# A two-layer FFN and adapter network on one core: part of the mixing done by quarters between product groups

## What is computed

```python
def L0_cond(x, weights, condition):
    return jnp.einsum('bct,bcd->bdt', x, weights[condition])        # x: (32, 64, 1024), weights: (16, 64, 64)
def L0_ffn(x, w12, b12, w3, b3):
    x1, x2 = jnp.split(jnp.einsum('bsk,mk->bsm', x, w12) + b12, 2, axis=-1)
    return jnp.einsum('bsm,nm->bsn', silu(x1) * x2, w3) + b3
def L1_cond(x, idx, W, lora_A, lora_B):
    xr = jnp.einsum('bsi,bir->bsr', x, lora_A[idx])
    return jnp.einsum('bsi,io->bso', x, W) + jnp.einsum('bsr,bro->bso', xr, lora_B[idx])
def L1_ffn(x, W_org, lora_down, lora_up, lora_keys, Wq):
    ...  # base product, softmax router over 8 experts, rank 64 each
x = x + L0_ffn(L0_cond(x, L0_cond_weights, itok), ...)
x = x + L1_ffn(L1_cond(x, itok, ...), ...)
```

## Time and profile before

| | us |
|---|---|
| median of 3 runs | 981.84 (981.64 to 982.62) |
| the profiled execution | 981.73 |
| its span | 980.0 |

### The profile page before, as it was taken

One profiled execution on the slowest core, in us unless ns is written; L12 is line 12 of the kernel. 1 busy time (PEld: TensorE's weight loads), 2 busy tenths in 40 slices (PEclk: granted clock), 3 DMA queues, 4 the chain that ended last, 5 costly groups with the idle time before them and its releaser, 6 DMA issues.

```text
span 980.0 us, 12537 instructions
## 1 busy us (share of the span) xinstructions
PE 975.1 (99%) x4790; PEld 807.9 (82%) x4790; DVE 799.2 (82%) x644; ACT 406.7 (41%) x373; POOL 37.7 (4%) x63
## 2 busy tenths in 40 slices
PE   9999999999999999999999999999999999999998
PEld 8888888888888888888898888888888888888886
DVE  3977877998867898778866888779987779887887
ACT  6553553453344433332355545444334453423322
POOL 2600000000000000000100000000000000000001
PEclk9999999999999999999999999999999999999999
DMA  9032044024013102240531210620340131012013
GB/s 353 2 100 94 1 160 183 20 81 179 24 44 119 53 1 65 97 162 11 192 142 43 86 44 9 236 99 28 116 159 1 43 129 44 1 65 86 1 44 129
DMA packets 23194, 84.43 MB, mean 86 GB/s; under 512 B 2706, under 2 KB 6818, under 8 KB 17250
## 3 DMA queue, kind: packets, MB, share of 16 engines
q1 hardware_dynamic: 20880, 75.77, 21.2%
q0 software_dynamic: 2112, 7.36, 1.9%
q10 hardware_dynamic: 146, 0.52, 0.2%
HBM read 75.25 MB, written 8.39 MB: 85 GB/s over the span
## 4 chain that ended last, share of the span: by engine, by line
PE 99%; DVE 0%; issue 0%
PE banks L695 32%; PE banks L696 31%; PE banks L697 31%; PE banks L787 3%; PE banks L751 1%; PE banks L770 1%; PE banks L821 0%; PE banks L800 0%; PE banks L816 0%; DVE r L1088 0%; DVE r L959 0%; PE banks L810 0%; PE banks L806 0%
## 5 line engine op out<-in xcount | busy, mean ns | idle before, releaser
L695 PE MATMUL banks<-s_hi,t_hi 128*128 128x512 f32 x1344 | 525.4, 391 | 0.0
L696 PE MATMUL banks<-s_lo,t_hi 128*128 128x512 f32 x1344 | 523.1, 389 | 0.0
L697 PE MATMUL banks<-s_hi,t_lo 128*128 128x512 f32 x1344 | 522.9, 389 | 0.0
L695 PEld LDWEIGHTS banks<-s_hi,t_hi 128*128 128x128 f32 x1344 | 252.2, 188 | 54.7 <-issue 1.5
L697 PEld LDWEIGHTS banks<-s_hi,t_lo 128*128 128x128 f32 x1344 | 252.3, 188 | 53.1
L696 PEld LDWEIGHTS banks<-s_lo,t_hi 128*128 128x128 f32 x1344 | 252.3, 188 | 51.1
L957 DVE TENSOR_TENSOR t_lo<-w,t_hi 128x1024 fp32r<-128x1024 f32 x134 | 160.0, 1219 | 9.4 <-ACT t_hi L890 9.4
L1083 DVE TENSOR_TENSOR r<-banks,r 128x1024 f32<-128x1024 f32 x102 | 123.5, 1220 | 46.3 <-PE banks L697 39.8
L890 ACT CAST t_hi<-w 128x1024 fp32r<-128x1024 f32 x134 | 136.5, 1048 | 51.2 <-PE banks L697 42.3
L862 ACT CAST s_hi<-st 128x2048 fp32r<-128x2048 f32 x40 | 76.5, 1913 | 183.0 <-PE banks L697 130.6
L957 DVE TENSOR_TENSOR s_lo<-st,s_hi 128x2048 fp32r<-128x2048 f32 x40 | 91.6, 2291 | 46.0 <-ACT s_hi L862 46.0
(11 more groups left out here) (84 smaller groups left out, 429.4 us busy)
## 6 DMA issues: line engine op xcount, KB each, us to landing
w<-w_up_in SPq DMA_DIRECT2D x16, 1024.0 KB, 5.0
w<-w_base_in SPq DMA_DIRECT2D x10, 1024.0 KB, 4.8
w<-w_down_in SPq DMA_DIRECT2D x8, 1024.0 KB, 5.1
r<-x_t_in SPq DMA_DIRECT2D x8, 1024.0 KB, 6.2
w<-w_lin_in SPq DMA_DIRECT2D x8, 1024.0 KB, 5.1
out_t<-r POOLq DMA_DIRECT2D x14, 512.0 KB, 4.8
we<-w_expin_in SPq DMA_DIRECT2D x10, 512.0 KB, 4.7
r<-x_pairs_in SPq DMA_DIRECT2D x8, 512.0 KB, 9.2
```

The source lines that it names most:

```text
L695: pe.matmul(out, w_hi, x_hi, start=start, stop=False, skip_group_check=True)
L696: pe.matmul(out, w_hi, x_lo, start=False, stop=False, skip_group_check=True)
L697: return pe.matmul(out, w_lo, x_hi, start=False, stop=stop, skip_group_check=True)
```

## The change

The mixing of pairs 6 and 7 of the first half, and of all pairs of the second, is done *by quarters* (`mixing_between`): each k is four matmuls, for the two samples j (rows 64j to 64j+63 of the array) and the two halves q of the 128 columns of x (PSUM partitions 64q to 64q+63), with 64 moving columns. Sample j goes to its own bank. The zero quarters of `mix` are no longer read.

Where it stands: the first half's pairs 6 and 7 come after group 1 of product 0; the second half's pairs two at a time after the last group of products 2, 3 and 5 of the first half's expup, and after group 2 of product 6. ACT's copies move along. Product 0 of the first half starts after pair 5; for this, the first two chunks' `s_hi` and `s_lo` are made ahead of the rest (`first_ready`). DVE makes the first half's sums T1 and T2 ahead of S1 and S2, and the second half's T1 and T2 within product 0 of its up0 and no longer beside the last expup product. SP loads x pairs 4 to 7 of the second half in a row, ahead of the weight block "12".

```diff
-    if n == 0:
-        to = 0
-    elif n < LAST and PRODUCTS[n + 1][1] == 0:
+    if kind == "up0" and i == 0:
+        to = s
+    elif n < LAST and PRODUCTS[n + 1][1] == 0 and kind_of(n + 1) != "up0":
         to = s + 1
...
+MIX_LATE = (6, 7)
+MIX_BETWEEN = {(2, 3): (0, 1), (3, 3): (2, 3), (5, 3): (4, 5), (6, 2): (6, 7)}
+def mix_bank(h, c):
+    return ((0, 2, 4, 6, 4, 6, 4, 6) if h == 0 else (4, 6, 4, 6, 0, 2, 0, 2))[c]
...
                 elif h + 1 < HALVES:
-                    load_x(h + 1, 4)
-                    load_x(h + 1, 5)
+                    for c in range(4, PAIRS):
+                        load_x(h + 1, c)
                     load_w(s + 1, "12")
-                    load_x(h + 1, 6)
-                    load_x(h + 1, 7)
                     load_w(s + 1, "22")
...
+            def mixing_between(h, pairs):
+                for c in pairs:
+                    bank = mix_bank(h, c)
+                    wait_mixing(h, c)
+                    if h == 0 or c in (2, 3, 6, 7):
+                        pe.wait_ge(mixed_copied, h * PAIRS + c - 1)
+                    else:
+                        wait_taken(pe, phase_of(h - 1, "expup", 1 if c < 4 else 4), 2 * (c % 2))
+                    for k in range(K):
+                        for q in range(2):
+                            for j in range(2):
+                                rows, cols = slice(j * S, (j + 1) * S), slice(q * S, (q + 1) * S)
+                                last = pe.matmul(banks[cols, bank + j, k * S:(k + 1) * S],
+                                                 x_pair(c)[rows, k * P + q * S:k * P + (q + 1) * S],
+                                                 mix[rows, c, rows], start=True, stop=True, skip_group_check=True)
                     last.then_inc(mixed_full, 1)
...
-                    pe.wait_ge(s_ready, n + 1)
+                    if n == 0:
+                        pe.wait_ge(first_ready, 1)
+                    else:
+                        pe.wait_ge(s_ready, n + 1)
...
+                        if n == 0 and p == 2:
+                            pe.wait_ge(s_ready, 1)
...
+                    if n == 0 and g == 1:
+                        mixing_between(0, MIX_LATE)
+                    if kind == "expup" and h + 1 < HALVES and (i, g) in MIX_BETWEEN:
+                        mixing_between(h + 1, MIX_BETWEEN[i, g])
...
+                between = kind == "expup" and h + 1 < HALVES
+                if between and i == 6:
+                    s_split(n + 1)
+                    copy_mixed(h + 1, 4)
+                    copy_mixed(h + 1, 5)
                 t_split(n, 0)
+                if between and i in (3, 4):
+                    for c in MIX_BETWEEN[i - 1, 3]:
+                        copy_mixed(h + 1, c)
+                if between and i == 6:
+                    copy_mixed(h + 1, 6)
+                    copy_mixed(h + 1, 7)
```

More of the change, by code:

```diff
@@ L825, in tensor_engine @@
                 h, kind = STAGES[s]
-                if kind == "up0" and i == 0:
-                    mixing(h)
+                if n == 0:
+                    mixing()
                 if kind == "lin" and i < 2:
@@ L862, in s_split, with t_split @@
                 act.copy(s_hi[:, slot, cols], s_source(n)).then_inc(s_hi_done, 1)
-            def t_split(beside, when):
+            def t_split(beside, when, which=(0, 1, 2, LORA)):
                 for n, j in t_halves(beside, when):
+                    if j not in which:
+                        continue
                     s, i = PRODUCTS[n]
@@ L951, in scalar_engine @@
                 t_split(n, 2)
-                if kind == "expup" and i == 6 and h + 1 < HALVES:
-                    mixing(h + 1)
+                if n == 0:
+                    for c in MIX_LATE:
+                        copy_mixed(0, c)
         def vector_engine(dve):
@@ L1178, in copy_coef @@
                                 coef_bank[:, 0:KE * BH]).then_inc(coef_ready, 1)
-            t_split(-1, 0)
-            s_split(0)
+            t_split(-1, 0, (0,))
+            slot, cols = s_place(0)
+            first, rest = slice(cols.start, cols.start + 2 * TN), slice(cols.start + 2 * TN, cols.stop)
+            dve.wait_ge(first_hi_done, 1)
+            lo(s_lo[:, slot, first], s_source(0)[:, 0:2 * TN], s_hi[:, slot, first]).then_inc(first_ready, 1)
+            dve.wait_ge(s_hi_done, 1)
+            lo(s_lo[:, slot, rest], s_source(0)[:, 2 * TN:], s_hi[:, slot, rest]).then_inc(s_ready, 1)
+            t_split(-1, 0, (1,))
             dve.wait_ge(consts_made, 5)
@@ L1199, in vector_engine @@
                     take(dve_own(n)[1])
-                    if i not in (3, 4):
+                    if i not in (3, 4) and (i < 6 or h + 1 == HALVES):
                         t_split(n, 0)
@@ L1230, in vector_engine @@
                     sum_y(s, 2)
+                if n == 0:
+                    for what in t_sums_beside(n):
+                        t_sum(*what)
                 for name in {0: ("S1", "S2"), 2: ("S4",), 3: ("S3",)}.get(i, ()):
```

80 lines of the change are left out of this document (51 added, 29 removed).

## The result

The changed kernel took 975.88 us in the median (975.6 to 976.59, six runs), the kernel before 981.82 in the same rounds. The ratio is 0.9939, with a 95% interval from 0.9926 to 0.9952: 6.0 us less, 0.6%. The forecast was 975.9, within a range from 974.4 to 982.0.

The account below looks back on a forecast made before the run. PE, busy 975.1 of 980.0 us, bounds the kernel. Removed mixing -17.9, quarters +9.5, places +2.0 and waits +0.5 give -5.9 us: 975.9 from 981.84, range 974.4 to 982.0.

Parts of the forecast that it names:

- What is removed: Full-size mixing on PE: the second half's eight pairs (14.29 us) and the first half's last two (3.60) go, 17.89 us.
- The price of a pair: Mixing by quarters: 0.95 us a pair if the step follows the columns, between 0.90 and 1.79; ten pairs 9.5 us.
- A place: Changing the array's shape around each of five places of two pairs: 0.40 us each (0.29 to 0.50), 2.0 us in all.
- Waits: PE waits at second pairs, the first product's start, product 2 and x loads: 0.5 us in all, bounds 0 and 1.5.
- The forecast's covers: Slack before PE would wait for DVE: 0.2 us at first product, 0.3 and 1.8 at product 2 of each half.
- The sum: Whole kernel: -17.9 + 9.5 + 2.0 + 0.5 = -5.9 us, from 981.84 to 975.9.
- Rival 1: Mixing quarters on PE: records, not columns, set the pace, 1.79 us a pair, +2.5 us, 984.3; chance 0.14.
- Rivals 2 and 4: Mixing quarters: a four at 0.07 to 0.09 us, 977.5 to 981 (0.15); or overlap only in twos, 984.3 or above (0.04).
- Rival 3: DVE late at product 2 of a half, or x pair 6 late, by 1 to 4 us: 977 to 980; chance 0.07.
- What would show it: New profile: 640 quarter records, places of 2.2 to 2.4 us, next half's product near 500.7; DVE waits would say otherwise.

Follow-up runs that it names:

- full_between: Changed kernel with its ten moved pairs as full 128x128 matmuls again, at the new places; 982.02 us, ratio 1.0001 to the kernel before.
- the two orders in turn: Changed kernel with its quarter matmuls reordered: all eight k of one quarter, then the next (997.13 us), or two quarters taking turns (982.76 us).
- all_quarters: Changed kernel with the first half's pairs 0 to 5 by quarters too and s_hi ahead of the weight cast; 981.91 us.
- one_place_quarters: Changed kernel with the second half's eight quartered pairs in one place after the last product, copies, sums and loads ordered as before; 982.5 us.
- one_place_quiet: one_place_quarters with the changed kernel's x loads, weight blocks 12 and 22 loaded after the last pair, weight sums in product 0; 980.38 us.
- weights_late: Changed kernel with the second half's weight blocks 12 and 22 asked for only after its last pair is mixed; 975.98 us, ratio 0.9927.
- halves_in_turn: Changed kernel with quarters two at a time, the two row halves in turn (order q, k, j); 982.76 us, ratio 0.9998.

## Why the prediction was right, step by step

- **What is removed**, 17.89 us: right in size. The first half gave 3.38 of its 3.60, since pair 4 began at 13.73 for 13.54, named as a wait for its load, which landed at 13.46 for 13.29. The changed kernel asks for these loads as before, and in the kernels here that keep pairs 0 to 5 at full size the same load landed between 13.12 and 14.19. So this is the execution and not the change.
- **The price of a pair**, 0.95 us between 0.90 and 1.79: measured 0.93. The argument was that L770 and L787 share a step because they share a stream, so that half the columns give half the step. full_between and the two orders in turn agree with both parts of it: the same matmuls give nothing at full size, and give it back when fewer quarters run together. The 55 ns for a weight load of 64 columns is only the columns' share: the record is 0.135 us long, as the rows of 32 and 128 columns would give (110 + 32 x 0.85 = 137 ns), so the loads fit under the step because they overlap.
- **A place**, 0.40 us between 0.29 and 0.50: measured 0.37, and 0.36 with one pair. Row halves and column halves together cost about what row halves cost alone in the earlier trace rows. The products behind a place were not in the sum, some 0.04 us each.
- **Waits**, 0.5 us between 0 and 1.5: about 0.8, and not where they were looked for. The forecast's covers held. DVE's half of s_lo was ready by 15.60 + 1.2 = 16.8, before PE came for it at 17.38; the t_lo of product 2 was ready at about 39.59 + 1.2 = 40.8 (forecast 40.9), and PE came at 41.4; that of the second half at 518.46 + 1.2 = 519.7 (forecast 520.7), and PE came at 521.9. X pairs 6 and 7 landed at 491.5 and 492.8, for a bound of 496.0, and PE wanted the first at 495.9. The 0.6 in the last place was missed: it is the late block of instructions, which the forecast had no term for.
- **The sum**: -17.9 + 9.3 + 1.9 + 0.2 (pair 4) + 0.6 (pause) + 0.2 (products behind the places) = -5.7, for a forecast of -5.9. Small misses of opposite sign nearly cancel: pairs and places cost 0.3 us less than forecast, the waits 0.3 and the products behind the places 0.2 more. That the medians differ by 6.0 and so meet the forecast to 0.1 us is luck.
- **Rival 1**, that the feed sets the pace: wrong at these places, where 128 matmuls take 1.87 us, 14.6 ns each. The Trainium skill ("TensorE: Matmul & The Clock Gate", section on the back-to-back issue gap) has about 25 ns as the least distance; the trace does not agree for matmuls that go to different quarters. But the rival was right about something that the forecast left out. A long run of quarters is fed one matmul each 28.6 ns, and the kernel before could not show whether that is a limit, since its densest row, L770, ran at 28 ns. What the forecast treated as one question, how fast the array takes small matmuls, is two: how fast it takes them, and how fast they reach it. The second counts only when a run goes on past the instructions in hand, here after 177 matmuls in one place and after 211 at the program's start. The places of 128, with products between them, stay below that: the placing brings nothing by itself, and the second half's quarters bring nothing without it. The forecast gave no such reason for its places of two pairs, so that they stay short enough is luck as far as its argument goes. The same terms gave the 975.9 expected of quarters in one place, which was wrong by 6.6 us.
- **Rivals 2 and 4**: a four at 0.058 us rules out both.
- **Rival 3**: no engine's or load's cover went.
- **What would show it**: 640 records, 2.24 us a place for 2.2 to 2.4, the next half's product at 500.13 for 500.7, and no DVE wait near 17, 41 or 522: as told, but for the one place of 2.85 and the 500.7. That figure is 491.51 + 4 x 2.3 and leaves out the 1.3 us that the forecast itself had won at the start (2 x 1.80 less one place of 2.3). With them it would have been 499.4, and 500.13 is 0.7 later: 0.6 for the pause, 0.2 for pair 4 and 0.2 for the products behind the places, less 0.3 for the cheaper pairs and places.

## What to carry over

The block-diagonal work of this kernel was worth cutting into quarters because consecutive matmuls fall on different quarters: the order inside the group decides between 0.93, 1.6 and 3.1 us for the same 64 matmuls. A group of small matmuls must be short enough for the instructions already in hand (here 128 gave at most a pause of 0.5 us, while long runs stopped after 177 and 211), with long matmuls before the next group; a place costs 0.37 us, so two pairs a place beat one. To price small matmuls in a trace of long ones, look for the instruction queue's packets as well as for PE's waits.

## What the runs showed of the hardware

- PE's instructions come in blocks of 16 KB (256 instructions). While PE waits for them in a long run of quarters one comes every 3.6 to 4.3 us, even with no other transfer (6.2 beside 400 GB/s of loads in all_quarters), and PE goes on 2.2 to 2.9 us after its packet's start. In one_place_quarters and one_place_quiet the next packet starts 1.33 to 1.35 us after PE has gone on. The trace shows the stop as idle time by "issue". One packet started about 1 us earlier when the weight loads were kept back (weights_late).
- Matmuls on four different 64x64 quarters start as little as 6 to 7 ns apart, and 128 of them, with 128 weight loads, take 1.87 us. A weight load's record is 0.135 us long there, so these overlap too. When one quarter's run follows another's, their edges overlap over about three records.
- The granted clock fell to 0.50 in the profiled executions of two kernels, during or behind stretches in which PE stood for want of instructions (one_place_quiet, all_quarters), and not in that of one_place_quarters, where PE stood for 6.7 us in all. But that was the fastest of ten: eight of them had a mean granted clock of 0.996 to 0.998, where those of the kernel before had 0.999 or 1.0. All eleven of all_quarters had 0.993 to 0.997. So such stops often came with a lower clock, and a small part of the 982.5 us may be that: the two executions at 1.0 took 982.04 and 982.14. What decides it is open.
- In four profiled executions the first mixing began at half its pace, 0.213 us a record for 0.112: until 10.87 us in halves_in_turn, 7.40 in weights_late, 7.06 in one_place_quarters and 6.89 in full_between. The traces' records of the granted clock begin 0.2 us behind these moments, at 11.05, 7.60, 7.30 and 7.12, and the row of the clock reads 1.00 for time without a record. So that row says nothing of the clock there; half a clock would fit, but no row shows it. The profiled execution of halves_in_turn took 984.72 us, the other seven 982.33 to 982.92.
